# Spreading the q and k features of a vision transformer's attention straight from their split tiles into q and k

## The reference, cut to what matters

```python
qkv = x @ w_attn + b_attn
q, k, v = jnp.split(qkv, 3, axis=-1)
q = q.reshape(Bx, Tx, NH, HS).transpose(0, 2, 1, 3)      # likewise k and v; NH = 12, HS = 16
att = jnp.einsum('bhqd,bhkd->bhqk', q, k) * (1.0 / math.sqrt(HS))
att = jnp.where(causal[None, None, :, :], att, -jnp.inf)
att = jax.nn.softmax(att, axis=-1)
y = jnp.einsum('bhqk,bhkd->bhqd', att, v)
```

## Time and profile before

| | us |
|---|---|
| median of 3 runs | 2377.52 (2372.65 to 2378.88) |
| the profiled execution | 2373.45 |
| its span, first to last instruction | 2371.7 |

### The profile page before, as it was taken

One profiled execution on the slowest core, in us unless ns is written; L12 is line 12 of the kernel. 1 busy time (PEld: TensorE's weight loads), 2 busy tenths in 40 slices (PEclk: granted clock), 3 DMA queues, 4 the chain that ended last, 5 costly groups with the idle time before them and its releaser, 6 DMA issues. The chain is left out here.

```text
span 2371.7 us, 49114 instructions
## 1 busy us (share of the span) xinstructions
PE 2143.0 (90%) x14772; PEld 2075.0 (87%) x14772; DVE 1591.5 (67%) x4304; ACT 1096.8 (46%) x2873; POOL 1561.6 (66%) x2294
## 2 busy tenths in 40 slices
PE   4999999999999999999999369999999999999950
PEld 4898998999999999999998369999999999999950
DVE  4577776877777777777767346666666666666646
ACT  2444444444444444444444135454544545454537
POOL 3356665767676767666665557777777777777743
PEclk9999999999999999999999679999999999999985
DMA  5657777776676656565643143201010110001338
GB/s 155 155 116 130 130 129 128 133 138 136 137 136 135 144 129 141 131 142 129 142 98 75 31 119 58 42 3 26 2 28 3 28 23 6 2 2 26 62 69 287
DMA packets 231952, 219.70 MB, mean 93 GB/s; under 512 B 90963, under 2 KB 212050, under 8 KB 230800
## 3 DMA queue, kind: packets, MB, share of 16 engines
q1 hardware_dynamic: 134512, 146.55, 25.6%
q10 hardware_dynamic: 43040, 56.78, 12.3%
q0 software_dynamic: 54272, 14.76, 5.0%
HBM read 152.91 MB, written 95.25 MB: 105 GB/s over the span
## 5 line engine op out<-in xcount | busy, mean ns | idle before, releaser
L1104 POOL DMA_INDIRECT x_tokens<-yout,e_entry x240 | 381.4, 1589 | 180.5 <-DVE yout L1251 134.2
L651 PE MATMUL Y<-p,vp 128*102 128x198 f32 x1536 | 362.1, 345 | 17.3 <-ACT ysb L482 12.0
L443 POOL DMA_INDIRECT expert_lists<-entry,slot x256 | 289.0, 1129 | 54.3 <-issue 54.3
L1266 DVE TENSOR_TENSOR a<-UP,gate 128x384 f32<-128x384 f32 x320 | 178.4, 558 | 217.7 <-ACT gate L1218 212.4
L487 ACT ACTIVATE p<-ST 128x396 f32<-128x396 f32 x384 | 191.4, 499 | 264.7 <-PE ST L623 254.8
L1173 PE MATMUL Y<-w,a_hi 128*128 128x384 f32 x960 | 304.4, 354 | 2.0 <-DVE a_lo L1256 2.0
L1084 POOL DMA_INDIRECT rows<-x_wide,e_entry x240 | 249.6, 1040 | 77.0 <-issue 72.1
L1218 ACT ACTIVATE gate<-GT 128x384 f32<-128x384 f32 x320 | 157.6, 492 | 295.9 <-PE UP L1160 295.9
L141 POOL TENSOR_TENSOR word_p<-word_p 1x1 f32<-1x1 f32 x416 | 86.5, 208 | 306.0 <-ACT p L489 297.2
L409 POOL TENSOR_TENSOR x_lo<-x,x_hi 128x396 fp32r<-128x396 f32 x192 | 208.0, 1085 | 89.3 <-ACT x_hi L465 87.4
L651 PEld LDWEIGHTS Y<-p,vp 128*102 128x102 f32 x1536 | 222.8, 171 | 32.1 <-issue 12.0
(11 more groups left out here) (182 smaller groups left out, 6326.7 us busy)
## 6 DMA issues: line engine op xcount, KB each, us to landing
x<-in_xt ACTq DMA_DIRECT2D x180, 198.0 KB, 4.8
q<-qk_features SPq DMA_DIRECT2D x384, 74.2 KB
k<-qk_features SPq DMA_DIRECT2D x192, 148.5 KB
qk_features<-qk_hi SPq DMA_DIRECT2D x96, 198.0 KB
qk_features<-qk_lo SPq DMA_DIRECT2D x96, 198.0 KB
e_raw<-in_wexp SPq DMA_DIRECT2D x8, 1408.0 KB, 6.3
rb<-rd ACTq DMA_DIRECT2D x128, 74.2 KB
t_x<-x_tokens SPq DMA_DIRECT2D x16, 576.0 KB, 5.1
```

Of the source, the lines that this page charges most:

```text
L443: pool.indirect_dma_start(d["lists"][:, :], bass.IndirectOffsetOnAxis(ap=slot[o][0:REAL[t], t, c:c + 1], axis=0), entry[o][0:REAL[t], t, c ...
L651: return pe.matmul(Y[0:VW1, 0:TI], v0, p32[b][:, hh, 0:TI], start=start, stop=stop)
L1104: pool.indirect_dma_start(d["x1"][:, :], row_of(cc, t), yout[q][:], None, bounds_check=N - 1, oob_is_err=False, compute_op=ALU.add)\
L1266: dve.tensor_tensor(a32[m % 2][:], UP[m % 2][:, 0:TILE3], gate[m % 2][:], ALU.mult)\
```

## The change

The array d["qk"] in HBM, its stores and their semaphores are gone. SP copies from qk_hi[t] and qk_lo[t] in SBUF into q and k in SBUF: for every image and tile t three DMAs of 96 source rows (spread_wide) and three of 32 source rows (spread_third), each row 198 floats (792 bytes). That is 18 DMAs an image. The weight columns are ordered so that the first 96 features of tile 0 are q of the even heads, of tile 1 q of the odd heads, of tile 2 k of the even heads, and the last 32 of each tile a third of k of the odd heads. Image 0's DMAs are issued at steps 3, 4 and 6 as each tile is ready, image 1's 18 at step 9. ACT, before it overwrites qk_hi[0], now waits on all 36 spreads of the pair before. The stores of x1 are 6 DMAs with both images in each, moved from step 8 of a body to step 0 of the next.

```diff
@@ SP
-            def store_qk(g, par, t):
-            def spread_q(par, im):
-            def spread_k(par, im):
...
+            def spread_wide(par, im, t):
+                cols = slice(im * TI, (im + 1) * TI)
+                for c, from_lo in enumerate(((0, 0, 1), (0, 0, 1), (0, 1, 0))[t]):
+                    row = 2 * HD * c + (HD if t == 1 else 0)
+                    dst = q[par][row:row + HD, im, t] if t < 2 else k[par][row:row + HD, im]
+                    src = (qk_lo if from_lo else qk_hi)[t][0:CH, cols]
+                    sp.dma_start(dst.bitcast(F32), src.bitcast(F32)).then_inc(s_qkr[im][par], 16)
+            def spread_third(par, im, t):
+                cols = slice(im * TI, (im + 1) * TI)
+                for c, from_lo in enumerate((0, 1, 0)):
+                    row = 2 * HD * c + HD
+                    src = (qk_lo if from_lo else qk_hi)[t][CH:P, cols]
+                    sp.dma_start(k[par][row:row + HD, im, 2 * t:2 * t + 2].bitcast(F32), src.bitcast(F32))\
+                        .then_inc(s_qkr[im][par], 16)
...
-                    if 1 in stages and s in (2, 3, 5):
-                        store_qk(g, par, (2, 3, 5).index(s))
-                    if s == 8 and 4 in stages:
-...
-                    if s == 7 and 1 in stages:
-                        wait(sp, s_st, (i - 2) * STEPS + 6)
-                        sp.wait_ge(s_qkw[par], (turn + 1) * (QW * 16))
-                        spread_q(par, 0)
-                        spread_k(par, 0)
+                    if s == 0 and 5 in stages:
+                        p = i - 4
+                        sp.wait_ge(s_x1, p + 1)
+...
+                    if s in (3, 4, 6) and 1 in stages:
+                        t = (3, 4, 6).index(s)
+                        if t == 0:
                             sp.wait_ge(s_qset, 5)
+                            wait(sp, s_st, (i - 2) * STEPS + 6)
+                        g.wait_drained(sp, f"QK{t}")
+                        spread_wide(par, 0, t)
+                        spread_third(par, 0, t)
                     if s == 9 and 1 in stages:
                         wait(sp, s_st, (i - 1) * STEPS)
-                        spread_q(par, 1)
-                    if s == 10 and 1 in stages:
-                        spread_k(par, 1)
+                        for t in range(3):
+                            spread_wide(par, 1, t)
+                            spread_third(par, 1, t)
@@ ACT, ahead of QK0
-                                wait(act, s_qkw[1 - par], (turn + par) * (QW * 16))
+                                for im in range(2):
+                                    wait(act, s_qkr[im][1 - par], (turn + par) * (QR * 16))
@@ host: columns of w_attn and b_attn
-    by_row = np.arange(C).reshape(NH // 2, 2 * HD).T.ravel()
-    order = np.concatenate([by_row, C + by_row, 2 * C + np.arange(C)])
+    by_row = np.arange(C).reshape(NH // 2, 2, HD).transpose(1, 2, 0)
+    thirds = C + by_row[1].reshape(HD, 3, 2).transpose(1, 0, 2)
+    wide = (by_row[0], by_row[1], C + by_row[0])
+    order = np.concatenate([np.concatenate([wide[t].ravel(), thirds[t].ravel()]) for t in range(3)]
+                           + [2 * C + np.arange(C)])
```

More of the change, by code:

```diff
@@ L281, in attention_block @@
         s_hhi, s_hlo, s_qkhi = sem("h_hi_part"), sem("h_split"), sem("qk_hi_part")
-        s_qkw = [sem("qk_stored0"), sem("qk_stored1")]
         s_qkr = [[sem(f"qk_spread{im}_{n}") for n in range(2)] for im in range(2)]
@@ L302, in attention_block @@
         SETS = 12
-        QW, QR = 6, 9
+        QR = 18
         def body_at(i):
@@ new lines, in spread_third, with rows_of @@
+            def spread_third(par, im, t):
[5 more added lines that the diff above has]
+                        .then_inc(s_qkr[im][par], 16)
+            def rows_of(name, p, hf):
+                view = d[name].rearrange("(n m t) c -> n t m c", m=2, t=T)
+                return view[p, hf * P:hf * P + REAL[hf]]
@@ L363, in body @@
                 for s in range(STEPS):
-                    n = (i - 1) * STEPS + s
-                    if 1 in stages and s in (2, 3, 5):
-                        if s == 2:
-                            wait(sp, s_s, (i - 1) * STEPS)
-                            sp.wait_ge(s_qset, 5)
-                        store_qk(g, par, (2, 3, 5).index(s))
-                    if s == 8 and 4 in stages:
[L371 to L378, removed]
@@ L379, in body @@
-                    if s == 7 and 1 in stages:
-                        wait(sp, s_st, (i - 2) * STEPS + 6)
-                        sp.wait_ge(s_qset, 5)
-                        sp.wait_ge(s_qkw[par], (turn + 1) * (QW * 16))
-                        spread_q(par, 0)
-                        spread_k(par, 0)
+                    if s == 0 and 5 in stages:
+                        p = i - 4
+                        sp.wait_ge(s_x1, p + 1)
+                        for hf in range(2):
+                            src = pay[par][0:REAL[hf], hf::2, :]
+                            x1_rows, xin_rows = rows_of("x1", p, hf), rows_of("xin", p, hf)
+                            for dst, part in ((x1_rows, src), (xin_rows[:, :, 0:C], src),
+                                              (xin_rows[:, :, C:XW], src[:, :, P:C])):
+                                sp.dma_start(dst, part).then_inc(s_st1[par], 16)
@@ L389, in body @@
-                    if s == 10 and 1 in stages:
-                        spread_k(par, 1)
+                        for t in range(3):
+                            spread_wide(par, 1, t)
+                            spread_third(par, 1, t)
             run_bodies(sp, body)
             for par in range(2):
-                sp.wait_ge(s_st1[par], NPAIR // 2 * 12 * 16)
+                sp.wait_ge(s_st1[par], NPAIR // 2 * 6 * 16)
         @block.gpsimd
@@ L549, in body @@
                                 done = turn - 2 + par
-                                act.wait_ge(s_st1[o], done * 12 * 16)
+                                act.wait_ge(s_st1[o], done * 6 * 16)
                                 act.wait_ge(s_sc[o], done * 8 * 16)
@@ L946, in body @@
                             done = turn - 2 + par
-                            dve.wait_ge(s_st1[o], done * 12 * 16)
+                            dve.wait_ge(s_st1[o], done * 6 * 16)
                             dve.wait_ge(s_sc[o], done * 8 * 16)
@@ L1404, in build @@
     d = dict(d)
-    d["qk"] = nc.dram_tensor("qk_features", [2, 2, 2, 2 * C, TI], F32).ap()
     d["x1"] = nc.dram_tensor("x1_tokens", [N, C], F32).ap()
```

## The result

The changed kernel takes 2404.47 us at the median of 13 runs (2384.42 to 2422.51), the kernel before 2378.88 beside it (2370.40 to 2388.12). The ratio is 1.0103, 95% interval 1.0077 to 1.0129: slower by about 24.5 us (0.0103 x 2378.88). The profiled execution of the changed kernel is the longest of its 13 (2422.51, span 2420.7). Its span lies 49 us over that of before (2371.7), twice the loss at the median, so its profile shows more of the loss than a usual run has. The times of the changed kernel spread over 38 us, those of before over 18.

What follows compares the result with a forecast made beforehand. PE, busy 97.42 of 100 us, was taken to bound the steady state. Profiled 2373.45 plus 15 us at the start gave 2388.5; plus 4.1 for the median, 2392.5, called 2392, range 2366 to 2422.

Steps and rivals of the forecast that it cites:

- Start: Pipeline start: ACT stands for the spreads at QK0 of the first pairs; 9 + 5 + 1 = +15 us.
- Issue of a spread: SP's spreads: 0.80 us plus a gap of 0.04 each, so 0.84; lower end 0.47, upper end 1.37.
- both copies of its kind lie there: Reason for 0.80: the only SBUF to SBUF copies with unlike shapes, q<-nm and rb<-rd, took 796 and 783 ns.
- Landing, 2.0 us: End of an image's spreads: data lands 2.0 us after the last issue.
- Steady state unchanged by the spreads: Attention block: spreads arrive 2 us early, SP's list takes 34 of 39.1 us a pair, so no change.
- Cost nothing if these come through: Stores of x1 at step 0, beside rb and nm of MX1: no cost if rb and nm are not delayed.
- rival 3: Stores of x1 make image 1's nm late, 4 us in one body of three: +40 us, near 2420; chance 0.08.
- The same bytes, half as many issues: Stores of x1: half as many DMA issues carrying the same bytes, taken to cost nothing.
- Moved to where SP is otherwise idle: Stores of x1: their new place falls where SP has nothing else to do, so no cost.
- Ports: Spreads' data: 84 GB/s onto 16 partitions, 10.9 us an image, less than 15.1 us of issues; no change.
- Rivals 1, 2 and 4: Spreads: issues of 0.47, 2373 (0.24); those with data bound at 84 GB/s, 2377 (0.08); SP's list the bound, 2473 (0.12).
- The gain from less traffic through HBM: Steady state: the way through HBM costs nothing; start: the shorter way gains about nothing of PE's 5.53 us stand.

Runs made afterwards that it cites:

- e3: Changed kernel with each 69-row store of x1 cut into 64 and 5 rows at step 0 (9 DMAs): 2376.81 us, ratio 1.0043.
- e12: Changed kernel with its six uncut stores of x1 issued at step 4, after image 1's nm has landed: 2376.21 us, ratio 1.0046.
- e7: Kernel before with its 69-row stores cut into 64 and 5 rows where they stand, at step 8: 2364.41 us, ratio 0.9999.
- e6: Changed kernel with 69-row stores cut into 64 and 5 at step 0, and spread semaphores split by tile: 2368.14 us, ratio 1.0014.
- e2: Kernel before with only the stores of x1 changed, to six at step 0 of the next body: 2372.62 us, ratio 1.0032.
- e8: Changed kernel with 19 extra DMAs of several kinds behind the attention block, on SP and ACT, to time an issue; whole time not compared.
- e1: Changed kernel with its stores of x1 back at step 8, in 12 DMAs: 2543.15 us, ratio 1.0764.
- e10: Changed kernel with 69-row stores of x1 cut into 67 and 2 rows at step 0 (9 DMAs): 2503.29 us, ratio 1.0579.
- e9: Changed kernel with spread semaphores split by tile, stores of x1 at step 7, 69 rows cut into 64 and 5: 2394.23 us, ratio 1.0119.

## Why the prediction was right or wrong

The number held: 2392 forecast with 2366 to 2422 around it, 2404.47 measured, and slower, which had 0.58. That is luck in good part, for the path to it did not hold. I had said +15 us from the start and nothing from the steady state. A start that I priced too high stood in for a loss that I had at nothing. By the runs it is this, from 24.5 us:
- nm beside the 69-row stores, 14 us (the changed kernel against e3 and e12, 0.0060 and 0.0057);
- the start, 4 us (QK0 of pairs 2 to 4, above);
- the steady bodies, 4 us. From QK0 of pair 12 to that of pair 28 is 624.6 us before and 624.8 in e7, but 627.2 in e3 and in e6, where nm is out of the way: 0.15 us more a pair, times some 28 pairs.

The last two make 8 of the 10 us that e3 still loses. What e2 loses (7.6 us) is no term of this sum, because its stores run at another moment.

Step by step.

**Issue of a spread: mis-sized.** 0.60 + 0.04 in place of 0.80 + 0.04. I had gone by "both copies of its kind lie there" and taken unlike shapes as what makes the kind. e8 says that the kind is wrong: a copy within SBUF costs 0.60 whatever its shape. The value taken was 0.84, the lower bound 0.47, and the truth lay between.

**Start: right mechanism, too large.** ACT did stand, and at QK0, as said: 11.71 us. But it had been ready earlier, since PE's first scores came at 53.64, not 57.0. The time lost at QK0 of pair 1 is 65.02 - 62.63 = 2.4 us, where I had 9.5, and no second stand followed. Put 0.64 into the same sum: image 0 is there at 39.9 + 11.5 + 2.0 = 53.4 (measured 53.64), image 1 at 51.4 + 11.5 + 2.0 = 64.9 (measured 65.02). The working was sound for both images; its one price carried the 15 us. It does not tell why the 2.4 us at pair 1 had become 3.9 at pair 2.

**Landing, 2.0 us: held,** by the same two numbers.

**Steady state unchanged by the spreads: nearly held.** SP's list is no bound, and ACT's wait costs nothing: in e3, where nm is out of the way, ACT stands at QK0 only once, at the start (12.0 us). But a pair takes 0.15 us longer, and this I had at nothing. The spreads also set when SP comes to the stores, as e2 shows.

**"Cost nothing if these come through": the step that failed.** I had named the place (rival 3: the stores run beside nm of MX1) and its price for a body (4 us), and gave it 0.08, because nm was waited for once in 64 in the kernel before. I had misread that one case. It was not only beside image 1's spreads. Its last two stores of 69 rows are these, 3.2 us ahead of nm at 364.60:

```profile
361.40 0.82 SPq L378 DMA_DIRECT2D x_wide<-pay  x2
```

In the body of rows 4 and 5 the stores end at 754.76 and nm is issued at 763.13, 8.4 us later. No other nm of that trace has a store of x1 in the 6 us ahead of it, and three of its twelve updates were the late ones, as in the changed kernel. So that row was a warning: the one time the stores stood there, nm was late. The chance was far too low. The price of rival 3 was a third of all bodies at 4 us each, 40 us. In the profiled execution, the longest, six bodies had a wait of over 3 us, and their pairs took 45.6 to 47.6 us from QK0 to QK0 in place of 39.3, together 42 us: fewer, and dearer. At the median it is worth 14. The bytes were the wrong measure too. "The same bytes, half as many issues" is true, and more DMAs of the same bytes, cut at 64 rows, are what cures it.

**"Moved to where SP is otherwise idle": too small a view of the edit.** e1 shows that in the old place they would cost 7.6%, since ACT's wait ahead of QK0 now stands behind them.

**Ports: not borne out.** From rb's 42 GB/s I had 84 for a copy onto 16 partitions, and called the partitions in play what sets the rate; no run shows that. e8 moves one at 169. The Trainium skill's figure (SBUF — State Buffer, Door 1: The DMA port swizzle), 104 GB/s for 16 neighbouring partitions, is below that too; here the measurement decides. Rb is slow for another reason, which I did not look for. Neither touched the sum, as issues take longer than data.

**Rivals 1, 2 and 4.** The issues were not 0.47, so neither of the first two came. SP's list did not become the bound in the changed kernel; it did in e1 and e10, by a wait and by standing in issues, not by the price of a spread.

**The gain from less traffic through HBM: none, as said.** PE's stands for it were 5.5 us before, and 3.6 of these were won.

What stays open. That the two share few DMA engines is read from the counts of late updates (three with 69 rows, one with 67) and of busy engines; which engines they are was not seen, nor why nm waits so long there (up to 10.5 us) for stores that SP has already issued. Nor why a steady pair takes 0.15 us more. This much of e6, the best version, it explains: e6 has lost both large costs and starts pairs earlier (QK0 of pair 2 at 86.70, before 89.93), yet is not faster than the kernel before (1.0014, 0.9997 to 1.0032), for it loses some 4 us again over the steady bodies. PE stands longer for ysb in it (20.4 us against 12.0 before); no run tells why.

## What to carry to other kernels

Ask of a moved DMA not how many bytes it has but what else runs in that moment and how its rows divide: 69 rows beside a small urgent transfer cost 14 us, the same rows as 64 and 5, or moved to step 4, cost none of that. Ask also what the list ahead of it now takes, because that sets the moment. A rare wait in the old trace is worth a look at what ran beside it before it is counted as rare. When a copy loses its way through memory, the buffer that it reads stays taken until the copy has landed; look for every engine that now waits for that, and let it wait for its own part only. Traffic that nobody waits for was worth nothing here when taken away.

## What the runs showed of the hardware that I had not expected

- Copies from SBUF to SBUF of three shapes (96 partitions onto 16, 128 onto 128, 16 onto 16) issued in 0.60 us at the median, on SP, and the first of them in 0.62 on ACT's queue (e8); nm's and rb's kinds took 0.82 and 0.76 on SP as well; loads and stores of HBM 0.36 to 0.47.
- Beside stores of 69 rows three of the twelve rows of nm landed late (up to 10.5 us after the issue, where it is 2.8 beside stores of 64 and 5), beside stores of 67 rows one (9.0 to 9.3).
- An engine can stand in the issue itself: 6.41 us for two stores and 5.68 for one in e10, with 0.06 of the DMA engines' time in use, against 0.83 to 1.86 for two in the bodies shown of the changed kernel.
- A load of x took 1.61 us to issue beside SP's 3.12 for two stores (e9), against 0.355 at the median.
- A copy onto 16 partitions moved at 169 GB/s (e8).
